# A megakernel's attention stage: the engines' loops over query tiles are written out straight, without branches

## The reference, cut to what matters

```
q = (x @ q_w.T).reshape(b, s, HEADS, HEAD_DIM).transpose(0, 2, 1, 3)
k = x @ k_w.T
v = x @ v_w.T
scores = jnp.einsum('bhqd,bkd->bhqk', q, k) * SCALE
attn = jax.nn.softmax(scores, axis=-1)
out = jnp.einsum('bhqk,bkd->bhqd', attn, v)
```

## Time and the profile before

| | us |
|---|---|
| median of 3 runs | 5529.28 (5528.55 to 5529.91) |
| the profiled execution, its own time | 5523.66 |
| its span, from the first to the last instruction | 5522.1 |
| first to last exponential of the attention stage (1097.57 to 2993.76) | 1896.19 |
| share of the full TensorE clock that was granted, whole span | 0.942 |

### The profile page before, as it was taken

How to read it: one execution, slowest core, us unless ns; L and a number is a source line. 1 busy time by engine, 2 the same in 40 slices (tenths; PEclk the granted TensorE clock), 3 DMA queues, 4 the chain that set the end, 5 groups by cost and what they waited for, 6 DMA issues and landing times. The chain is left out here.

```text
span 5522.1 us, 103884 instructions
## 1 busy us (share of the span) xinstructions
PE 5049.2 (91%) x33816; PEld 3716.9 (67%) x33817; DVE 3037.6 (55%) x4906; ACT 2193.5 (40%) x4377; POOL 2191.6 (40%) x1498
## 2 busy tenths in 40 slices
PE   4999978999999999999999869999499988877999
PEld 3788866655555555555555558888499966657999
DVE  7222227577777777777773652222556566855454
ACT  3122222165555565555554312222443322324443
POOL 2344513066666666666664035443211024421000
PEclk7999987799999999999999979999799998888999
DMA  5223327300000000000001623332523211113111
GB/s 168 75 91 100 99 88 244 116 16 13 16 13 16 16 13 16 16 13 16 14 16 51 202 81 98 94 93 81 159 91 95 90 64 36 57 59 97 46 46 39
DMA packets 218268, 380.33 MB, mean 69 GB/s; under 512 B 27282, under 2 KB 81682, under 8 KB 217364
## 3 DMA queue, kind: packets, MB, share of 16 engines
q1 hardware_dynamic: 185172, 264.13, 14.7%
q0 software_dynamic: 32704, 111.17, 7.0%
HBM read 253.05 MB, written 121.63 MB: 68 GB/s over the span
## 5 line engine op out<-in xcount | busy, mean ns | idle before, releaser
L1252 DVE TENSOR_REDUCE attend_mx<-attend_am_ps 128x1 f32<-128x1024 f32 x1024 | 1220.4, 1213 | 512.0 <-PE attend_am_ps L1143 511.5
L1242 POOL TENSOR_TENSOR attend_pairs<-attend_pt 128x1024 f32<-128x1024 f32 x512 | 1219.3, 2381 | 706.3 <-ACT attend_pt L1227 706.3
L1227 ACT ACTIVATE attend_pt<-attend_sc_ps 128x512 f32<-128x512 f32 x2048 | 1113.6, 595 | 811.7 <-PE attend_sc_ps L1132 789.3
L1132 PE MATMUL attend_sc_ps<-attend_qst,attention_kst 98*128 98x512 f32 x2048 | 839.0, 450 | 37.9 <-issue 28.3
L1143 PE MATMUL attend_am_ps<-attention_kst,attend_qst 96*128 96x512 f32 x2048 | 669.8, 410 | 9.1 <-DMA attend_qst<-q_parts 5.7
L1132 PEld LDWEIGHTS attend_sc_ps<-attend_qst,attention_kst 98*128 98x128 f32 x2048 | 348.2, 190 | 455.7 <-ACT attend_pt L1227 237.0
L1161 PE MATMUL attend_pv_ps<-attend_pt,attention_v 128*32 128x256 f32 x8192 | 556.2, 389 | 0.4 <-ACT attend_pt L1227 0.4
L669 DVE TENSOR_TENSOR expert_ac<-expert_gu_ps,expert_gl 128x512 f32<-128x512 f32 x144 | 99.7, 692 | 669.7 <-ACT expert_gl L633 669.7
L1143 PEld LDWEIGHTS attend_am_ps<-attention_kst,attend_qst 96*128 96x128 f32 x2048 | 395.0, 195 | 96.4 <-DVE attend_mx L1252 22.3
L1652 DVE SCALAR_TENSOR_TENSOR ffn_hf<-ffn_gu_ps,ffn_us,ffn_sg 128x256 f32<-128x256 f32 x352 | 170.7, 485 | 396.5 <-ACT ffn_sg L1599 396.5
L1536 PE MATMUL ffn_gu_ps<-ffn_y_hi,ffn_wg_hi 128*128 128x256 f32 x1408 | 355.1, 284 | 15.3 <-DVE ffn_y_lo L808 12.4
(11 more groups left out here) (384 smaller groups left out, 9480.7 us busy)
## 6 DMA issues: line engine op xcount, KB each, us to landing
weights_raw<-experts_dram POOLq DMA_DIRECT2D x76, 512.0 KB
ys<-expert_ob SPq DMA_DIRECT2D x144, 256.0 KB
attend_qst<-q_parts SPq DMA_DIRECT2D x192, 128.0 KB
yn<-route_yb SPq DMA_DIRECT2D x64, 256.0 KB
ffn_xb<-x SPq DMA_DIRECT2D x64, 256.0 KB
ffn_rb<-x SPq DMA_DIRECT2D x64, 256.0 KB, 3.0
weights_raw<-experts_dram SPq DMA_DIRECT2D x24, 512.0 KB
route_xb<-x_dram SPq DMA_DIRECT2D x32, 256.0 KB
```

The costliest lines, as they stand in the source:

```text
L1132: pe.matmul(sc[:, g, :], kst[0:KROWS + 2, b * S + kt * P:b * S + (kt + 1) * P], qst[0:KROWS + 2, k, hh:hh + 4, :], start=True, stop=True). ...
L1227: act.activation(pt[:, u % RING, g * 4 * P:(g + 1) * 4 * P], sc[:, g, :], ACT.Exp, scale=HD ** -0.5).then_inc(p_rdy, 1)
L1242: pool.tensor_tensor(pairs[:, p % PRING, :], pt[:, 2 * p % RING, :], pt[:, (2 * p + 1) % RING, :], ALU.add).then_inc(pair_rdy, 1)
L1252: dve.tensor_reduce(mx[:, u // 2, u % 2:u % 2 + 1], am[:, u % 2, :], AX.X, ALU.max).then_inc(mx_rdy, 1)
```

## The change

`rounds` no longer makes a loop. All 32 tiles are written out, for all five engines, with the same arguments that the loops gave: tile number n, buffer n % 2, pair n // 2, batch, and the batch of the tile whose maxima are made (none for the last). Every n is now a constant.

```
         def rounds(eng, step):
-            for k in range(2):
-                step(k, k, 0, 0, 0)
-            for b in range(B):
-                with eng.Fori(0 if b else 1, QT // 2 - 1) as i:
-                    for k in range(2):
-                        step(i * 2 + (k + b * QT), k, i + b * (QT // 2), b, b)
-                for k in range(2):
-                    n = (b + 1) * QT - 2 + k
-                    step(n, k, n // 2, b, b if k == 0 else (b + 1 if b + 1 < B else None))
+            for n in range(N):
+                last = n + 1 == N
+                step(n, n % 2, n // 2, n // QT, None if last else (n + 1) // QT)
```

## The result

The changed kernel takes 5442.05 us in the median (5440.12 to 5446.27, 6 runs), the kernel before 5529.80 (5528.55 to 5530.32, 6 runs). The ratio is 0.9845, with an interval of 0.9835 to 0.9855: 1.55% faster. The forecast was 5446 us, range 5438 to 5460. The profiled execution took 5442.26 us, against 5523.66 before.

What follows compares the result with a forecast made beforehand. TensorE was taken to bound the kernel, busy 91% of the span. Branches (51.5 us), pace (31.7) and seams (0.3), 83.4 us in all, came off the median of 5529.28 us, giving 5446, range 5438 to 5460.

Steps and rivals of the forecast that it cites:

- TensorE bounds the stage and the stage gives its gain to the kernel: Attention stage: TensorE is busy without a break in a tile, and time leaving the stage, 83.4 us, leaves the kernel.
- From the profiled time to the median: Whole kernel: the median lies 5.6 us above the profiled run, so 5440.3 us profiled becomes 5446.
- The written-out tile: Attention stage: every tile written out takes 56.64 us, as tile 14 already did in the trace before.
- The branches: TensorE's attention loops: 11 taken branches cost 51.5 us in idle time, slower clock and restart, all of which goes.
- The pace: Attention loop tiles without a branch: 57.86 us against 56.64 written out, 1.22 us a tile, 31.7 us for 26.
- The seams: Tiles 1 and 15, running into a loop's first waits, lose 0.15 us each; written out they gain 0.3 us.
- Straight code is brought in time: TensorE's attention code, grown to 33,000 instructions, is fetched without delay; priced at nothing.
- Rival C: Attention stage: straight code starves TensorE, 244 us more than the straight pace, time 5690 us; chance 0.03.
- A: Attention stage: only the branches go, tiles stay at 57.86 us; saving 51.5 us, time 5478; chance 0.05.
- D: Whole kernel: no visible change, the attention gain is given back, for instance by a lower clock; time 5529 us; chance 0.03.
- The size of the body as the reason for the dear branch: TensorE's loops: a taken branch over 920 instructions is cheap, one over 2250 dear, with instruction memory holding 2048.
- The later stages, priced at nothing: Stages after attention: their loops move in memory, none of their 42 branches took over 0.242 us; priced at nothing.

Runs made afterwards that it cites:

- tensor_straight: The kernel before with only TensorE's tiles written out, the other four engines still looped; 5486.27 us, ratio 0.9913.
- scalar_moved: tensor_straight plus 128 already-met waits in ScalarE's written-out tiles 14 and 15, which move its second loop; 5478.95 us, one run.
- scalar_straight: The kernel before with only ScalarE's tiles written out, the other engines still looped; 5495.81 us, one run.
- others_straight: The kernel before with all engines but TensorE written out, TensorE still looped; 5487.95 us, ratio 0.9913.
- wide_loop: The kernel before, loops kept, each group of four 32-wide TensorE products made one 128-wide product, layer's output left out; 5402.48 us, one run.
- compact: The kernel before with TensorE alone written out, ScalarE's loop at one tile a turn and its score wait last there; 5439.67 us, ratio 0.9847.

## Why the prediction was right, point by point

**TensorE bounds the stage and the stage gives its gain to the kernel.** Right: 83.15 us left the stage, and 81.4 the profiled execution.

**From the profiled time to the median.** The sum gave 5440.3 us for the profiled execution, which took 5442.26. Then 5.6 us were added, because the median before lay so far above its profiled run. That difference had no cause to rest on, and it did not repeat: the changed kernel's median, 5442.05, lies 0.2 us below its profiled run. This term, and not the stage, is why the forecast of 5446 is 4 us too high.

**The written-out tile.** Forecast 56.64 us from two tiles, measured 56.63 in tiles 1 to 30. The forecast for the stage was 1812.8 us and it took 1813.04. That six tiles of the trace before were already in the new form made this nearly a reading.

**The branches, 51.5 us for 11.** The sum is right, one account of it was not. It held that TensorE's branch was all of it, since ScalarE's and VectorE's rows show 0.045 to 0.056 us. TensorE's is the main part: 11 idle times of 2.4 to 3.2 us and the clock behind them. But in the second loop ScalarE's own return costs it 2.5 us or more six times. Alone (tensor_straight against scalar_moved's cure) that is about 1 us a turn of the loop. Beside TensorE's branch it was hidden: by the prediction's sum an edge of the second loop, 27.2 / 6 = 4.5 us, cost no more than one of the first, 24.3 / 5 = 4.9. This is a part of why the savings do not add. tensor_straight's stage is 43 us shorter than the 1895.4 and 1896.2 of the kernel before, scalar_straight's 29, together 72, and the two in one 83. Of the 11 us between, ScalarE's returns, which tensor_straight lays bare, are 6; the loop tiles of tensor_straight, at 57.93 us, are 2; the rest is that the eleven edges cost 55 us in scalar_straight. With the 36 us of others_straight, where they cost 48, the sum is 79.

**The pace, 1.22 us a tile, 31.7 us.** The size is right (57.86 against 56.63 in the changed kernel). The place was left open between ScalarE and TensorE; it is ScalarE, and there one register instruction that stands between the score's arrival and the exponential, not the 94 a tile that the prediction counted.

**The seams, 0.3 us.** Tiles 1 and 15 take 56.63 us like the rest, 0.17 less than before. Right.

**Straight code is brought in time.** Right: no idle time of TensorE in thirty tiles. Rival C has nothing for it, A falls with 56.63 us in every tile, D with the stage's 83 us.

**The size of the body as the reason for the dear branch.** Right in kind: wide_loop makes it cheap with all engines' loops and waits in place. The two counts were a little low: by the trace a turn in the feed-forward layer has 954 instructions and one in attention 2300, for the prediction's 920 and 2250. The bound between them is now 1148 to 1916.

**The later stages, priced at nothing.** The span outside attention is 3625.9 and 3627.8 us in two profiles of the kernel before, and 3627.7 and 3632.1 in two of the changed one. tensor_straight has 3634.2 and compact 3623.3, and both move the later stages as well. So it varies by some 11 us, and kernels with moved code stand at both ends of that. That also covers the difference between 83 us in the stage and 87.75 between the medians, whose interval reaches from 80 to 91 us. An effect of the move in memory of a few us can't be told from that, for better or worse.

## What to carry to other kernels

Look whether the trace already holds the form that a change would make: tiles written out at a loop's ends are a measurement of the loop's price. A loop's price sits in two places. One is the return, where the body is long or lies badly, so keep a body short on the engine that bounds the stage (1148 instructions returned for 0.2 us on TensorE, 1916 for 3.8), and read what comes after the branch, not only the branch's row. The other is any instruction between a semaphore's rise and the work it releases. Of several waits ahead of one instruction, let the one that comes last in time be the one that the instruction itself carries: last in the source where counts are registers, first where they are constants, as this compiler placed them.

## What the runs showed of the hardware that was not expected

A taken branch shows its cost differently by engine: on TensorE in the branch's own record (3.4 to 4.5 us), on ScalarE as nothing in the record (0.045 us) and 2.4 to 3.1 us before the next instruction, on GpSimd in the same way with 2.9 to 4.0 us. The same 354 instructions on ScalarE returned in 0.2 us in one place and 2.5 us in another, and 128 instructions put ahead of them were enough to change it. An idle time of TensorE of 2.6 to 3.2 us cost its tile between 2.8 and 6.1 us, by what the granted clock did about its end. In others_straight and scalar_straight it was 2.8 to 3.0 us where the clock stayed at 2.4 GHz (5 of 22), 4.1 to 4.4 where it fell to 1.2 GHz for 3.4 us, and 5.6 to 6.1 where it fell for 6.8 us. The kernel before had such a fall behind 10 of its 11 branches in one profile and behind all in the other. Why some leave it out is open. In thirty unbroken tiles, 1.7 ms, the clock stayed at 2.4 GHz.
